# Four graph layers on one core: two float32 products in place of rounded ones, one shared set of statistics, and a longer software pipeline in the last stage

## The reference, cut to what matters

```python
# layer 2: aggregate, two-layer MLP with a batch norm after each product
agg = einsum('nm,bmd->bnd', A_hat, x)
h   = relu(batchnorm(agg @ W1.T))          # 128 -> 256, statistics over all rows
out = batchnorm(h @ W2.T)                  # 256 -> 128, statistics over all rows
x   = layernorm(x + out)
# layer 3: three mixings of the nodes (diagonal, upper, lower part of adj), one weight each
out = sum(einsum('ij,bjo->bio', adj_k, x @ W3[k]) for k in range(3)) + bias
x   = layernorm(x + out)
```

## Time and profile before

| | us |
|---|---|
| median of 3 runs (lowest, highest) | 1807.09 (1803.0, 1809.46) |
| profiled execution, its time | 1812.38 |
| its span | 1810.7 |
| busy in the span: PE, DVE, ACT, POOL | 1527.2, 1406.5, 1071.6, 560.5 |

### The profile page before, as it was taken

How to read it: one execution, slowest core, us unless ns; L and a number is a source line. 1 busy time by engine, 2 the same in 40 slices (tenths; PEclk the granted TensorE clock), 3 DMA queues, 4 the chain that set the end, 5 groups by cost and what they waited for, 6 DMA issues and landing times. The chain is left out here.

```text
span 1810.7 us, 29462 instructions
## 1 busy us (share of the span) xinstructions
PE 1527.2 (84%) x9302; PEld 1266.1 (70%) x9364; DVE 1406.5 (78%) x3257; ACT 1071.6 (59%) x2019; POOL 560.5 (31%) x764
## 2 busy tenths in 40 slices
PE   3998999899899999948999999999976775777775
PEld 3888888788888888836777777777754444555554
DVE  3578777777777777767888888888857886888886
ACT  3675676566566657626666666666633444666664
POOL 2122212212122221223333333333336773333333
PEclk9999999999999999969999999999988998888888
DMA  2000000000000000000000000000000000111111
GB/s 89 1 1 24 12 1 13 24 8 6 15 22 1 12 24 1 1 14 7 19 18 17 12 17 17 17 12 17 17 18 12 0 0 24 59 58 58 58 58 47
DMA packets 19516, 37.60 MB, mean 21 GB/s; under 512 B 3312, under 2 KB 4848, under 8 KB 19312
## 3 DMA queue, kind: packets, MB, share of 16 engines
q1 hardware_dynamic: 18576, 34.49, 5.9%
q10 hardware_dynamic: 864, 2.11, 0.3%
HBM read 19.81 MB, written 16.78 MB: 20 GB/s over the span
## 5 line engine op out<-in xcount | busy, mean ns | idle before, releaser
L378 PE MATMUL banks<-early_rounded 128*128 128x128 f32 (+3 forms) x1424 | 457.5, 321 | 64.1 <-DVE early_rounded L991 31.3
L379 PE MATMUL banks<-early_rounded 128*128 128x128 f32 (+3 forms) x1424 | 453.2, 318 | 0.0
L380 PE MATMUL banks<-early_rounded 128*128 128x128 f32 (+3 forms) x1424 | 452.7, 318 | 0.0
L796 ACT ACTIVATE early_scratch<-banks,consts 128x256 f32<-128x256 f32 (+2 forms) x624 | 312.3, 566 | 130.1 <-PE banks L380 115.8
L378 PEld LDWEIGHTS banks<-early_rounded 128*128 128x128 f32 x1424 | 279.2, 196 | 89.4 <-issue 41.8
L379 PEld LDWEIGHTS banks<-early_rounded 128*128 128x128 f32 x1424 | 279.5, 196 | 14.4
L380 PEld LDWEIGHTS banks<-early_rounded 128*128 128x128 f32 x1424 | 279.2, 196 | 13.8
L646 POOL CAST early_rounded<-early_scratch 128x512 fp32r<-128x512 f32 (+2 forms) x160 | 94.0, 597 | 551.2 <-DVE early_scratch L986 551.2
L488 POOL TENSOR_TENSOR consts<-consts 128x4 f32<-128x4 f32 (+1 forms) x112 | 125.9, 1124 | 158.8 <-DVE consts L462 156.3
L378 PE MATMUL banks<-kept_rounded 128*128 128x128 f32 (+2 forms) x384 | 142.1, 370 | 28.2 <-POOL kept_rounded L706 11.8
L750 ACT ACTIVATE attention_rounded<-banks 32x512 fp32r<-32x512 f32 (+1 forms) x160 | 94.5, 591 | 98.4 <-PE banks L1343 67.9
(11 more groups left out here) (169 smaller groups left out, 3459.1 us busy)
## 6 DMA issues: line engine op xcount, KB each, us to landing
early_scratch<-in_x_dram SPq DMA_DIRECT2D x16, 512.0 KB, 3.6
x_away<-attention_scratch SPq DMA_DIRECT2D x32, 256.0 KB, 2.0
late_scratch<-x_away SPq DMA_DIRECT2D x32, 256.0 KB, 2.7
out_dram<-late_scratch SPq DMA_DIRECT2D x32, 256.0 KB, 2.0
x_all<-in_WihT_dram ACTq DMA_DIRECT2D x1, 1024.0 KB, 5.5
x_all<-in_WhhT_dram ACTq DMA_DIRECT2D x1, 768.0 KB, 7.3
x_all<-in_Wqkv_dram ACTq DMA_DIRECT2D x1, 192.0 KB, 10.2
kept_scratch<-in_W_dram SPq DMA_DIRECT2D x1, 192.0 KB, 2.4
```

The source lines that it names most:

```text
L378: pe.matmul(out, wt[0], mv[0], start=start, stop=False)
L379: pe.matmul(out, wt[1], mv[0], start=False, stop=False)
L380: return pe.matmul(out, wt[0], mv[1], start=False, stop=stop)
L796: nc.scalar.activation(gate_f[lane][gate][:, 0:cols], bank(bank_set("lstm", n, unit), gate)[:, 0:cols], ACT.Tanh if gate == G else ACT.Sig ...
```

## The change

The W2 product of the MLP pass and the sum over the three weights of layer 3 become plain float32 matmuls on `hid_f` and `mix_f`, so that the splits before them go; `w2` and `w3` are no longer split. The mixing stays three rounded products. The remainder of the MLP input moves from POOL to DVE. In the last stage the statistics of the third and the fourth layer norm are worked out together, the third of group k with the fourth of group k-4, in one set of small operations and one power on POOL; the remainder of x3 moves from POOL to DVE; nearly all buffers become two deep (`x3_f` four); and the order goes by `late_groups`, with four heads in a loop body.

The core of the diff:

```diff
+    def late_groups(eng, order, do):
+        def head_of(head, at):
+            for what, part, late in order:
+                if not isinstance(head, int) or 0 <= head - late < GROUPS:
+                    do(what, part, head - late, (at - late) % 4)
...
@@ POOL
-            def second_pass(i, u): ...     # remainder of the MLP input
-            def hidden_low(i, u): ...      # remainder of the second half of hid_f
...
             def do(what, part, g, place):
+                pool.wait_ge(late_var, g + 1)
+                wait_if(pool, out_ready, g - 5)
+                wait_if(pool, x3_kept, min(g - 1, GROUPS) if isinstance(g, int) else g - 1)
+                nc.gpsimd.tensor_tensor(rstd[:, lo:hi], var[:, lo:hi], minus_half[:, lo:hi], ALU.pow)\
+                  .then_inc(late_rstd, 1)
+                pool.wait_ge(late_rstd, g + 1)
+                    nc.gpsimd.tensor_tensor(shift_cols[:, (place % 2) * GB:(place % 2) * GB + GB],
+                                            mean[:, GB:2 * GB], rstd[:, GB:2 * GB], ALU.mult).then_inc(shift4, 1)
@@ ACT
-                    wait_if(act, hid_lo, g * 2)
+                    wait_if(act, w2_sums, g - 1)
...
                 if what == "mixed":
                     act.wait_ge(mixed, g * GB + part + 1)
-                    wait_if(act, w3_sums, g)
+                    wait_if(act, w3_sums, g - 1)
-                    copy(mix_r[0][:, at:at + 3 * P], banks[:, 2 + part, 0:3 * P]).then_inc(mixed_hi, 1)
+                    copy(mix_f[place % 2][:, at:at + 3 * P], banks[:, 2 + part, 0:3 * P]).then_inc(mixes_kept, 1)
...
                 if what == "norm":
-                    act.wait_ge(shift4, g + 1)
+                    act.wait_ge(shift4, g + 5)
...
-            groups(act, [("x3", 0, 2), ("sums", 0, 3), ("scaled", 0, 0), ("mixed", 0, 2), ("mixed", 1, 2), ("mixed", 2, 2), ("mixed", 3, 2), ("norm", 0, 3)], do, pairs=3)
+            late_groups(act, [("norm", 0, 5), ("sums", 0, 4), ("scaled", 0, 0), ("mixed", 0, 3), ("mixed", 1, 3), ("mixed", 2, 3),
+                              ("x3", 0, 2), ("mixed", 3, 3)], do)
@@ DVE
-            def agg_high(i, u): ...
-            def hidden_parts(i, u): ...
+            def agg_parts(i, u):
+                wait_if(dve, w1b_sums, (g - 2) * 2 + 2)
+                nc.vector.tensor_copy(agg_r[u][0], xcols(g)).then_inc(aggb_hi, 1)
+                dve.wait_ge(aggb_hi, g + 1)
+                nc.vector.tensor_tensor(agg_r[u][1], xcols(g), f32(agg_r[u][0]), ALU.subtract).then_inc(aggb_lo, 1)
...
+            def low_third(g, place):
+                dve.wait_ge(x3_hi, g + 1)
+                nc.vector.tensor_tensor(x3_r[place % 2][1], x3_f[place], f32(x3_r[place % 2][0]),
+                                        ALU.subtract).then_inc(x3_lo, 1)
+
+            def late_round(k, at):
+                third = not isinstance(k, int) or k < GROUPS
+                fourth = not isinstance(k, int) or k >= 4
+                if fourth:
+                    ins = add_fourth(k - 4, at)
+                if third:
+                    ins = add_third(k, at)
+                ins.then_inc(late_work, 1)
+                if not isinstance(k, int) or 1 <= k <= GROUPS:
+                    norm_third(k - 1, (at - 1) % 4)
+                statistics(k, third, fourth, at)
+                if not isinstance(k, int) or 1 <= k <= GROUPS:
+                    low_third(k - 1, (at - 1) % 4)
@@ PE
             def second_layer(i, u):
-                pe.wait_ge(hid_lo, g * 2 + 2)
                 wait_if(pe, z_kept, g - 1)
-                mm3(pe, out, cut(w2_r, 0, P), cut(hid_r[u], 0, GC), stop=False)
-                mm3(pe, out, cut(w2_r, P, 2 * P), cut(hid_r[u], GC, 2 * GC), start=False).then_inc(w2_sums, 1)
+                for m in range(2):
+                    pe.wait_ge(hid_kept, g * 2 + m + 1)
+                    ins = pe.matmul(banks[:, 4 + u, :], raw2["w2"][:, m * P:(m + 1) * P], hid_f[u][m], start=m == 0,
+                                    stop=m == 1)
...
                 if what == "sums":
-                        ins = mm3(pe, by_batch(banks[:, 1, :], GB), cut(w3_r, k * P, (k + 1) * P), mixes,
-                                  start=k == 0, stop=k == 2)
+                        ins = pe.matmul(by_batch(banks[:, 1, :], GB), raw2["w3"][:, k * P:(k + 1) * P],
+                                        mixes[:, :, k, :], start=k == 0, stop=k == 2)
...
-            groups(pe, [("mix", 2, 3), ("mix", 3, 3), ("sums", 0, 3), ("back", 0, 3), ("mix", 0, 2), ("turn", 0, 0), ("mix", 1, 2)], do, pairs=3)
+            late_groups(pe, [("sums", 0, 4), ("mix", 0, 3), ("mix", 1, 3), ("mix", 2, 3), ("mix", 3, 3), ("back", 0, 4),
+                             ("turn", 0, 0)], do)
```

More of the change, by code:

```diff
@@ L218, in groups @@
                     do(what, part, head - late, (head - late) % 2)
+    def late_groups(eng, order, do):
[3 more added lines that the diff above has]
+                    do(what, part, head - late, (at - late) % 4)
+        warm = 8
+        for head in range(warm):
+            head_of(head, head)
+        with eng.Fori(warm // 4, GROUPS // 4) as i:
+            for at in range(4):
+                head_of(i * 4 + at, at)
+        for head in range(GROUPS, GROUPS + max(late for _, _, late in order)):
+            head_of(head, head)
     ctx = ExitStack()
@@ L333, in gnn_stack @@
         mid.close()
[L336 to L345, removed]
+        f3 = Area(sb("late_scratch", 21 * GC))
+        mix_f = [f3.take(GB * 3 * P) for _ in range(2)]
+        z_f, oT_f = f3.take(GC), f3.take(GC)
+        y3 = [f3.take(GC) for _ in range(2)]
+        y4 = [f3.take(GC) for _ in range(2)]
+        x3_f = [f3.take(GC) for _ in range(4)]
         o_f = [f3.take(GC) for _ in range(2)]
         x2_back = [f3.take(GC) for _ in range(2)]
+        hid_f = [[y3[u], y4[u]] for u in range(2)]
+        late_small = f3.take(2 * 12 * 2 * GB)
         x2_away = nc.dram_tensor("x2_away", [P, B, P], F32, kind="Internal").ap()
@@ L495, in ln_apply, with late_cols @@
             return ins
+        def late_cols(u):
+            t = late_small[:, u * 24 * GB:(u + 1) * 24 * GB]
+            st = t[:, 0:12 * GB].rearrange("q (b k) -> q b k", k=6)
+            return [st] + [t[:, (12 + 2 * j) * GB:(14 + 2 * j) * GB] for j in range(5)]
         xg_copied, x_turned, xT_hi, xT_lo = sem("xg_copied"), sem("x_turned"), sem("xT_hi"), sem("xT_lo")
@@ new lines, in add_fourth @@
+            def add_fourth(g, place):
+                st = late_cols(place % 2)[0]
+                dve.wait_ge(o_turned, g + 1)
+                wait_if(dve, out_ready, g - 1)
+                nc.vector.tensor_tensor(y4[place % 2], banks[:, 6, :], x3_f[place], ALU.add).then_inc(y4_made, 1)
+                dve.wait_ge(y4_made, g + 1)
+                for b in range(GB):
+                    ins = nc.vector.bn_stats(st[:, GB + b, :], y4[place % 2][:, b * P:(b + 1) * P])
+                return ins
@@ L1226, in _ @@
+            for k in range(8):
+                late_round(k, k % 4)
+            with dve.Fori(2, GROUPS // 4) as i:
+                for at in range(4):
+                    late_round(i * 4 + at, at)
+            for k in range(GROUPS, GROUPS + 4):
+                late_round(k, k % 4)
         @block.tensor
```

201 lines of the change are left out of this document (89 added, 112 removed).

## The result

The changed kernel takes 1865.32 us (median of 4 runs, 1865.12 to 1868.78), the kernel before on the same chip 1808.28 (4 runs): the ratio is 1.032, with a 95% interval from 1.0294 to 1.0346. Slower by 57 us, where +70 was forecast. The profiled execution took 1868.78 us, with a span of 1867.0.

The account below looks back on a forecast made before the run. TensorE was taken to bound the MLP pass (-37 us) and a loop of waits through DVE, POOL and ACT the last stage (+107); +70 on the profiled 1812.4 gives 1882, less 5.3: 1877 us, range 1844 to 1914.

Parts of the forecast that it names:

- The MLP pass: MLP pass: TensorE decides, 3.13 us a group with float32 matmuls at 0.86; 105.4 us for 142.3, -37.
- rival 2: MLP pass: a float32 matmul of 512 columns costs 0.47 us, pass -62, kernel 1852 us; chance 0.12.
- The ring: Last stage: each round waits in a loop, DVE statistics, POOL, ACT `norm` to x3 rounding, DVE remainder; stage +107 us.
- Its signs: Last stage profile: DVE idle some 7 us ahead of L1244, ACT some 7 us ahead of its first L914.
- Rival 1: Last stage: no loop, engine load decides; rounds 6.2 to 6.5 us, stage -67, kernel 1703 us; chance 0.07.
- Its length: Last stage: loop of 12.7 us a round from DVE 5.6, POOL 2.07, ACT 4.7, hand-overs 0.2; bounds 12.3 and 14.
- The 28 periods: Last stage: rounds 5 to 32 have the whole loop, round 32 lacks 2.2 us; 353.4 us.
- the lead-in: Last stage, ahead of the 28 periods: first rounds, a stop and a first loop passage; 33 us.
- the tail: Last stage, behind the 28 periods: last ACT heads, statistics, power, normalization and store; 24 us.
- Elsewhere: Outside the two stages: attention's early groups lose splits, nothing to -2 us, taken as nothing.
- rival 3: Last stage: TensorE joins the loop at the lower clock, a round of 13.5 us, kernel 1900 us; chance 0.13.
- Sum: Whole kernel: -37 in the MLP pass and +107 in the last stage give +70 us, 1877 us.

Follow-up runs that it names:

- The products doubled: Changed kernel with the two plain float32 W2 matmuls of each MLP group issued twice: 1921.51 us, ratio 1.0623 to the kernel before.
- `norm` last: Changed kernel with `norm` moved from first to last in ACT's head in the last stage: 1696.55 us, ratio 0.9368 to the kernel before.
- the run with the MLP pass alone: Kernel before with only the changed kernel's MLP pass, its last stage as before: 1768.68 us, ratio 0.9776 to the kernel before.
- the doubled run: Changed kernel with the three float32 products for w3 issued twice per group in the last stage: 1870.85 us, ratio 1.0341 to the kernel before.
- x3 first: Changed kernel with ACT's rounding of x3 moved to the front of its head, `norm` right behind: 1816.84 us, ratio 1.0045 to the kernel before.

## Why the prediction was right

- **The MLP pass.** Forecast 105.4 us with 3.13 a group, measured 104.4 and 3.12; -37 forecast, -37.9 measured. The ends took 4.6 us for 5.2, though 12 matmuls of 0.63 and not 0.40 are 2.8 more and not the 2.4 that the prediction adds. A plain float32 matmul of 512 columns is two records of 0.43, 0.86 us, as taken from the earlier trace rows. That settles rival 2 (0.47): it is out. The 0.94 us of four passes at the rounded pace of 0.235 is out too, by 5 us over the pass. The Trainium skill (FP8 and Floating Point Precision, section TensorE Precision Notes) gives true FP32 four passes and no time for one. Nothing here speaks against its four: 0.86 is four times 0.215, and two records a matmul agree with it if each holds two passes, which no row shows. The products doubled show that TensorE decides.
- **The ring.** Its members and their order were right; moving the three copies out moves the round by what they hold, and moving `norm` opens the ring. Its signs came where they were looked for: DVE idle 6.86 us ahead of L1244, ACT 7.44 ahead of L914. No later row passed a waiting one: DVE's L1226 had what it waits for when TensorE's turn back was done (1648.42 + 0.66 = 1649.08) and started only at 1651.35, behind L1244. The Trainium skill (TensorE: Matmul & The Clock Gate, the section on the 16 sub-arrays) calls ACT and DVE strict FIFO, and these rows agree. Rival 1 is what the kernel becomes with `norm` last: 1696.55 us, beside the 1703 given for it.
- **Its length.** Forecast 12.7, measured 12.14 to 12.22 in the four full rounds ahead of the loop body and 12.35 on average in it, where DVE's hand-over to POOL takes 0.22 to 0.24 us for 0.08 and POOL's to ACT mostly 0.12 for 0.03. In the round shown: DVE 5.52 (5.6 taken); POOL 1.64 + 0.07 + 0.20 = 1.91 (2.07); ACT from L914 to the end of the rounding 4.56 (4.7), of it the three copies 1.11 for 1.23; hand-overs 0.37 (0.2). The row for the power of 8 columns was of another stage and 0.15 too long. The 28 periods took 1844.32 - 1503.08 = 341.2 us for 353.4 (the last two, of 11.58 and 9.21, lost 3.9 together and not 2.2), the lead-in 32.0 for 33, the tail 22.7 for 24. Stage +92.6 for +107: the mechanism right, and the stage 395.9 us for 410.4, all three terms 3 to 6% too large.
- **Elsewhere.** Nothing to -2 was forecast, +1.7 measured, -2.2 in the run with the MLP pass alone. Kernels with nearly the same instructions there differ by 4 us; no run was made for the cause, and it stays open.
- **TensorE at the lower clock (rival 3)** was half right. The clock fell, to 0.77 on average, and the six records of the round shown took 5.34 us, most of them 0.85 apart, where 2.84 is the full pace of 0.43 a record. But the round doesn't follow: in the changed kernel itself the six records took 2.84 us in the round from 1737.14 and up to 5.49 in others, while all rounds of the loop last 12.27 to 12.40, that one 12.39. And 7.5 us of twelve records in the doubled run left the round as it was.
- **The cast.** The prediction read 0.74 us beside POOL out of the earlier trace rows. That is the mean of two casts in one row, 1.14 and 0.41; it changed no term, since it took 0.43 for the pass without POOL.
- **Sum.** -37.9 + 92.6 + 1.7 = +56.4 of span, for +70. What would have made the kernel faster, the case that the prediction gave 0.07, is one entry of ACT's list.

## What to carry to other kernels

When a change rewrites the order of two or more queues, walk every wait from engine to engine for one round, and see whether you come back to where you started within the same round; then add up the ring before you add up the loads. An item whose input comes late belongs at the end of its engine's round, with nothing behind it that the others wait for: moving `norm` there was worth some 170 us, four times the MLP pass's gain. A low busy share on all engines at once, with three waits that name each other in a circle, is what such a ring looks like in a profile, and doubling the work of an engine is a cheap test of whether it is in it (some 5 us outside, 79 inside).

## What the runs showed of the hardware that was not expected

- The granted clock of TensorE rose when it got more work: 0.77 in the last stage of the changed kernel with 267 us busy, 0.88 with 315 us busy in the same length, and 0.96 with 191 busy of 224 in the kernel with `norm` last. Within the changed kernel's stage it goes back and forth between its two levels, 1.2 and 2.4 GHz, so that the same six records take 2.84 us in one round and 5.49 in another.
- POOL's power of 8 columns took 1.88 to 2.09 us in all 28 rounds of the run with x3 first, where DVE's L1244 was already running when it started (1600.76 and 1600.99: 1.95), and 1.63 to 1.64 in the changed kernel, where DVE stood still. Where L1244 started after it (1601.58 behind 1600.99 with `norm` last) it took 1.63. So it is not having DVE beside it that costs, but finding it at work, and not at any work: the power of 4 columns took 1.48 us at 1479.00 of the changed kernel, with L1244 running, and 1.02 at 1475.77 with the addition L1215 running, where 1.01 is its time alone. L1215 reads one operand from `banks` and L1244 none; that this is what decides, no run here shows.
- DVE's cast of 512 columns is 0.41 us with POOL idle. In the MLP pass of the kernel before the 30 casts of a hidden tile (L1146) that ran beside POOL's remainder L706 took 0.97 to 1.16 us, the 34 others 0.41 to 0.43. That is a saving on DVE that no edit of its own makes: it comes with POOL's leaving the pass.
